# Turning the attended heads with VectorE's 32x32 block transposes, in a kernel of one gated attention stack

## The reference

```
x = x + tanh(g_xattn[0]) * divergence_attention_and_MLP(layernorm(x), ctx)      # phase a
x = x + tanh(g_ffn[0])   * linear(fp8(layernorm(x)), fp8(weight))               # phase b
x = x + tanh(g_xattn[1]) * attention(layernorm(x), ctx, mask, 16 heads of 16)   # phase b
x = x + tanh(g_ffn[1])   * (h + 0.5 * (silu(layernorm(h) @ w1 + b1) @ w2 + b2)) # phase b

# the attention, for each batch:
scores = q @ k.T / 4, where(mask == 0, -1e9); attn = softmax(scores)
out    = (attn @ value) by heads -> [256 tokens, 256] @ w_o.T + b_o
```

## Time and profile before

| | us |
|---|---|
| three runs: median (lowest to highest) | 1618.51 (1613.52 to 1624.93) |
| profiled execution, first to last instruction | 1614.4 |
| phase b in it | from about 600 on |
| one iteration with all eight letters | 27.8 |
| PE busy over the span | 1486.5 (92%) |
| DVE busy over the span | 1316.4 (82%) |
| ACT, POOL busy over the span | 1135.2, 1034.7 |

### The profile page before, as it was taken

One profiled execution on the slowest core, in us unless ns is written; L12 is line 12 of the kernel. 1 busy time (PEld: TensorE's weight loads), 2 busy tenths in 40 slices (PEclk: granted clock), 3 DMA queues, 4 the chain that ended last, 5 costly groups with the idle time before them and its releaser, 6 DMA issues.

```text
span 1614.4 us, 42641 instructions
## 1 busy us (share of the span) xinstructions
PE 1486.5 (92%) x14155; PEld 1144.6 (71%) x14155; DVE 1316.4 (82%) x3187; ACT 1135.2 (70%) x2057; POOL 1034.7 (64%) x1392
## 2 busy tenths in 40 slices
PE   4999999999999972668999999999999999999997
PEld 2788888888888861435667676777777776777666
DVE  4698888888888875778988889898988889898742
ACT  7798888888888742355666666666666666676664
POOL 4588888888888744224556565665656566565445
PEclk9999999999999995588999999999999999999999
DMA  7322222322222002332223232232223232232200
GB/s 228 96 80 66 91 72 65 96 66 69 93 65 71 2 1 92 80 119 73 80 80 87 73 85 80 85 87 81 83 78 92 72 91 74 86 85 84 64 16 22
DMA packets 197690, 125.45 MB, mean 78 GB/s; under 512 B 44400, under 2 KB 196848, under 8 KB 197360
## 3 DMA queue, kind: packets, MB, share of 16 engines
q1 hardware_dynamic: 197616, 124.48, 26.2%
HBM read 92.69 MB, written 25.17 MB: 73 GB/s over the span
## 4 chain that ended last, share of the span: by engine, by line
PE 48%; SPq 4%; DVE 3%; issue 2%; DMA 2%; POOL 2%; ACT 1%; POOLq 0%
PE b_bank L1835 28%; PE b_bank L1910 7%; PE b_scoreT L1892 4%; PE b_score L1875 4%; PE b_bank L1843 2%; PE b_bank L1987 1%; SPq L1306 1%; DMA b_nmT<-b_nm 1%; DMA b_yT<-b_y 1%; SPq L1290 1%; DVE b_nm L1653 1%; SPq L1279 1%; PE b_bank L1925 1%; ACT b_E L1471 1%; SPq L1315 0%
## 5 line engine op out<-in xcount | busy, mean ns | idle before, releaser
L1471 ACT ACTIVATE b_E<-b_scoreT 128x1024 f32<-128x1024 f32 x256 | 262.2, 1024 | 152.5 <-PE b_scoreT L1892 151.3
L1653 DVE TENSOR_REDUCE b_nm<-b_score 128x4 bf16<-128x1024 f32 x256 | 313.3, 1224 | 54.6 <-PE b_score L1875 48.4
L31 ACT ACT_TABLE_LOAD x157 | 201.4, 1283 | 18.6 <-PEq L1059 15.2
L1835 PE MATMUL b_bank<-f,b_YT 128*128 128x256 bf16 x1536 | 190.3, 274 | 4.7 <-POOL b_YT L1404 4.6
L890 PE MATMUL bank<-hT,W1T 128*128 128x256 bf16 x1536 | 183.3, 273 | 2.4 <-DVE hT L706 1.7
L1835 PE MATMUL b_bank<-b_hT,f 128*128 128x256 bf16 x1536 | 183.4, 273 | 0.8 <-DVE X L1749 0.8
L890 PE MATMUL bank<-W2T,G 128*128 128x256 bf16 x1024 | 171.0, 272 | 6.7 <-DVE GT L780 6.2
L1835 PEld LDWEIGHTS b_bank<-f,b_YT 128*128 128x128 bf16 x1536 | 143.5, 98 | 39.7 <-issue 19.5
L1835 PEld LDWEIGHTS b_bank<-b_hT,f 128*128 128x128 bf16 x1536 | 147.7, 98 | 30.3 <-issue 12.6
L890 PEld LDWEIGHTS bank<-hT,W1T 128*128 128x128 bf16 x1536 | 148.0, 98 | 27.7 <-ACT G L549 4.0
L1388 POOL TENSOR_TENSOR b_v<-b_v,b_e 128x512 f32<-128x512 f32 x32 | 40.6, 1269 | 195.0 <-DVE b_e L1734 195.0
(11 more groups left out here) (222 smaller groups left out, 3524.8 us busy)
## 6 DMA issues: line engine op xcount, KB each, us to landing
b_Q<-q_dram SPq DMA_DIRECT2D x192, 64.0 KB, 2.6
b_K<-k_dram SPq DMA_DIRECT2D x192, 64.0 KB, 2.8
xin<-in_x SPq DMA_DIRECT2D x32, 256.0 KB, 3.2
ctxn<-in_ctx SPq DMA_DIRECT2D x32, 256.0 KB, 2.8
mask_in<-in_mask SPq DMA_DIRECT2D x32, 256.0 KB, 3.0
X<-in_x SPq DMA_DIRECT2D x32, 256.0 KB, 4.0
ctxt<-in_ctxT SPq DMA_DIRECT2D x32, 256.0 KB, 4.2
b_ctxt<-in_ctxT SPq DMA_DIRECT2D x32, 256.0 KB, 2.8
```

Of the source, the lines that this page charges most:

```text
L31: act.add_instruction(mybir.InstLoadActFuncSet(name=nc.get_next_instruction_name(), act_func_set_id=which, ins=[], outs=[]))
L1471: nc.scalar.activation(E[:, pair:pair + 2], scoreT_ps[:, :, :, :], ACT.Exp).then_inc(sig["E"], 1)
L1653: nc.vector.tensor_reduce(pair, score_ps[:, :, :, :], AX.X, ALU.max, negate=True).then_inc(sig["nm"], 1)
L1835: last = nc.tensor.matmul(out_tile, lhs(i, k), rhs(j, k), start=start and k == chunks[0] and (i, j) == TERMS[0], stop=stop and k == chunks ...
```

## The change

The PE transposes of the attended heads and ACT's copies ahead of them go. DVE turns the tiles itself, in blocks of 32x32, out of PSUM (`heads_turned`), takes reciprocals and multiplies in SBUF (`inverse_sums`, `attended`), and turns the product back with a second block transpose (`heads_back`, tile `oF`). The rows of w_o and b_v are reordered on the way in so that the new order of the features fits. Half 0 of this is done in the iteration in which the batch is letter a, half 1 begins at the end of that iteration and ends in the next. Further, `statistics_2` stands ahead of maxima(5), `mlp_normalised` after maxima(6) of the iteration before, `scaled` right ahead of `binades`, `mask_bias` one letter earlier, and on POOL `inverse_std_2` ahead of `silu_parts`. The load of the mask goes from between the two steps on maxima to just behind the transposing transfers of `yT`.

```diff
             7: [("xT", "xlo", L_QKV, 1, 1), ("Q", "qlo", L_QKV, 1, 1), ("FFN", "ob", L_FFN, 1, 1),
                 ("PROJ", "x3", L_PROJ, 1, 1), ("H0", "Y", L_MLP, 4, 1), ("V", "V", L_QKV, 1, 1)],
-            8: [("OT0", "on", L_PROJ, 2, 1), ("hT", "hlo", L_MLP, 1, 1), ("ON", "onlo", L_PROJ, 1, 1),
-                ("AV01", "oS", L_ATT, 2, 1), ("H1", "Y", L_MLP, 4, 2)],
-            9: [("OT1", "on", L_PROJ, 2, 2), ("K", "klo", L_QKV, 1, 1), ("AV23", "oS", L_ATT, 2, 2),
-                ("H3", "Y", L_MLP, 4, 4)],
+            8: [("hT", "hlo", L_MLP, 1, 1), ("AV01", "at", L_ATT, 2, 1), ("H1", "Y", L_MLP, 4, 2)],
+            9: [("K", "klo", L_QKV, 1, 1), ("AV23", "at", L_ATT, 2, 2), ("H3", "Y", L_MLP, 4, 4)],
         }
...
                 if q:
+                    load_mask()
                     spill_queries()
...
                 if m:
                     transpose_maxima()
-                if q:
-                    load_mask()
...
-                if h:
-                    silu_parts(h, 0)
                 if f:
                     inverse_std_2()
                 if h:
+                    silu_parts(h, 0)
                     silu_parts(h, 1)
...
                 def attended_high():
-                    act.wait_ge(sig["onT_mm"], done(o))
+                    act.wait_ge(sig["oF"], done(o, per=C))
...
-                    nc.scalar.activation(oT[:, 0], whole_bank(BANK["ON"]), ACT.Copy).then_inc(sig["onhi"], 1)
-
-                def heads_copy(g):
...
+                    nc.scalar.activation(oT[:, 0], oF[:, :, :], ACT.Copy).then_inc(sig["onhi"], 1)
...
+                def heads_turned(c):
+
+                    dve.wait_ge(sig["av_mm"], done(a, per=NH // HG, part=2 * c + 2))
+                    nc.vector.transpose(at[:, 2 * c:2 * c + 2].rearrange("p g b r -> p (g b r)"),
+                                        flat_bank(BANK[("AV01", "AV23")[c]])).then_inc(sig["at"], 1)
+
+                def inverse_sums(c, b):
+                    dve.wait_ge(sig["at"], done(b, per=C, part=c + 1))
+                    nc.vector.reciprocal(rsum[:, 2 * c:2 * c + 2, :], at[:, 2 * c:2 * c + 2, :, DK]).then_inc(sig["rsum"], 1)
+
+                def attended(c, b):
+                    dve.wait_ge(sig["rsum"], done(b, per=C, part=c + 1))
+                    nc.vector.tensor_tensor(on[:, c].rearrange("p b g d -> p g b d"), at[:, 2 * c:2 * c + 2, :, 0:DK],
+                                            rsum[:, 2 * c:2 * c + 2, :].rearrange("p g (b u) -> p g b u", u=1).to_broadcast(
+                                                [P, 2, Q32, DK]), ALU.mult).then_inc(sig["on"], 1)
+
+                def heads_back(c, b):
+
+                    dve.wait_ge(sig["on"], done(b, per=C, part=c + 1))
+                    if (due := done(b, back=1)) is not None:
+                        dve.wait_ge(sig["onhi"], due)
+                    nc.vector.transpose(oF[:, c, :], on[:, c].rearrange("p b g d -> p (b g d)")).then_inc(sig["oF"], 1)
...
-                if h:
-                    mlp_normalised()
-                if n:
-                    scaled()
                 if o:
-                    attended(0)
+                    inverse_sums(1, o)
                 if m:
                     maxima(0)
+                if o:
+                    attended(1, o)
                 if q:
                     normalised_low()
                 if o:
-                    attended(1)
+                    heads_back(1, o)
...
                 if n:
+                    scaled()
                     binades()
...
+                if f:
+                    statistics_2()
                 if m:
                     maxima(5)
+                if a:
+                    heads_turned(0)
+                if m:
                     maxima(6)
+                if a:
+                    inverse_sums(0, a)
+                if o:
+                    mlp_normalised()
+                if a:
+                    attended(0, a)
                 if w:
                     result()
-                if f:
-                    statistics_2()
-                if m:
+                if a:
+                    heads_back(0, a)
+                if q:
                     mask_bias()
+                if m:
                     maxima(7)
                 if f:
                     attention_normalised()
+                if a:
+                    heads_turned(1)
...
-                if o:
-                    heads_transposed(0)
                 if m:
                     scores(0)
-                if o:
-                    heads_transposed(1)
...
-                if o:
-                    attended_transposed()
```

More of the change, by code:

```diff
@@ L1556, in iteration @@
                     exponential(6)
-                    heads_copy(0)
                     exponential(7)
@@ L1562, in iteration @@
                     silu(1)
-                if a:
-                    heads_copy(1)
                 if h:
@@ L1622, in mask_bias @@
                 def mask_bias():
-                    dve.wait_ge(sig[f"mask{m.parity}"], landed(m))
-                    if (due := done(m, back=2, per=NP)) is not None:
+                    dve.wait_ge(sig[f"mask{q.parity}"], landed(q))
+                    if (due := done(q, back=2, per=NP)) is not None:
                         dve.wait_ge(sig["scoreT_mm"], due)
-                    nc.vector.tensor_scalar(mb[m.parity][:, :, :], mask_in[:, :, :], 0.0, MINUS, ALU.is_equal,
+                    nc.vector.tensor_scalar(mb[q.parity][:, :, :], mask_in[:, :, :], 0.0, MINUS, ALU.is_equal,
                                             ALU.mult).then_inc(sig["mb"], 1)
                 def mlp_normalised():
-                    dve.wait_ge(sig["rs3"], done(h))
-                    if (due := done(h, back=1)) is not None:
+                    dve.wait_ge(sig["rs3"], done(o))
+                    if (due := done(o, back=1)) is not None:
                         dve.wait_ge(sig["hT_mm"], due)
                     for t in range(T):
-                        last = nc.vector.tensor_scalar(hn[:, t, :], Xb(h, t), mv3[:, t, 0:1], rh3[:, t:t + 1], ALU.subtract,
+                        last = nc.vector.tensor_scalar(hn[:, t, :], Xb(o, t), mv3[:, t, 0:1], rh3[:, t:t + 1], ALU.subtract,
                                                        ALU.mult)
@@ L1693, in keys_low @@
                     last.then_inc(sig["klo"], 1)
[L1695 to L1703, removed]
-                                            rsum[:, t, :].rearrange("p (h u) -> p h u", u=1).to_broadcast([P, NH, DK]),
-                                            ALU.mult).then_inc(sig["on"], 1)
+                def heads_turned(c):
+                    dve.wait_ge(sig["av_mm"], done(a, per=NH // HG, part=2 * c + 2))
+                    nc.vector.transpose(at[:, 2 * c:2 * c + 2].rearrange("p g b r -> p (g b r)"),
+                                        flat_bank(BANK[("AV01", "AV23")[c]])).then_inc(sig["at"], 1)
@@ L1797, in iteration @@
                     attention_update()
-                if m:
-                    maxima(5)
-                    maxima(6)
-                if w:
-                    result()
                 if f:
@@ L1980, in values_in @@
                     row_projection("V", 2, cT, "V_mm")
-                def heads_transposed(t):
-                    free(f"OT{t}")
-                    pe.wait_ge(sig["oS"], done(o, per=2))
-                    dst = flat_bank(BANK[f"OT{t}"])
-                    for g in range(NH // HG):
-                        last = nc.tensor.transpose(dst[:, tile(g)], oS[:, g, tile(t)], ident[:, :])
-                    last.then_inc(sig["oT_mm"], 1)
-                def attended_transposed():
-                    free("ON")
-                    pe.wait_ge(sig["on"], done(o, per=T))
-                    transposed(bank[BANK["ON"]], on, "onT_mm")
                 def output_projection():
@@ L2098, in col, with by_heads @@
         return np.ascontiguousarray(np.reshape(inputs[name], (-1, P)).T)
+    def by_heads(rows):
+        grid = np.reshape(rows, (2, 2, 4, DK, -1))
+        return np.ascontiguousarray(np.reshape(np.transpose(grid, (0, 2, 1, 3, 4)), (NH * DK, -1)))
     arrays = {
```

23 lines of the change are left out of this document (12 added, 11 removed).

## The result

| | before | after |
|---|---|---|
| median of four runs each (lowest to highest), us | 1617.62 (1613.52 to 1624.93) | 1677.42 (1675.11 to 1680.17) |
| profiled span, us | 1614.4 | 1673.2 |
| iterations with all eight letters, two lengths in turn, us | 27.80 and 27.93 | 29.98 and 30.2 |

The changed kernel is slower: ratio 1.0363, 95% interval 1.0333 to 1.0393. The forecast was 1663 us. Iterations of two lengths take turns in both kernels, and the forecast took the shorter one of before for all. The means are 27.87 and 30.1 us; the second length of before is seen from 1126.77 to

A forecast was written before the change was run, and what follows sets the result against it. PE bounds the kernel at 27.8 us an iteration; a loop of 29.4 + 0.2 = 29.6 us replaces it, 45 us over 25 iterations, hence 1663 us. Own range 1645 to 1685 (0.60); 8 in 10: 1622 to 1702.

The forecast's parts named there:

- the loop: Through bank 9: DVE's last transpose, `hidden(3)`, `values_in`, scores(0), maxima(0), DVE's work; 29.4 us, 29.6 with collisions.
- the second term: DVE from maxima(0) to the end of the last transpose: 26.0 less 0.27 for the reciprocal, 25.7 us.
- the 2.06 I kept: `xh` on DVE, two instructions beside POOL's work, assumed to take 2.06 us as before.
- 0.1 each: Loss of `attended` and `attended_low` to POOL, now reading both operands from SBUF: 0.2 us together.
- +3 and -4: Partly filled iterations: some 3 us more in neighbours of full ones, some 4 us back in the last.
- DVE's work, 26.0 us: DVE's work per iteration: 24.5 + 1.2 + 0.6 for block transposes - 0.3 for `v`'s new place.
- PE's, 26.3: PE's work per iteration: 27.8 us less 1.5 us of head transposes.
- `statistics_2` earlier ... costs nothing: On DVE: the move takes away the 1.4 us wait for `rs` and was costed at nothing.
- PE idle ahead of the fp8 matmuls: PE would wait some 0.8 us for `yT`, its way there being 1.5 us shorter and SP's not.
- PE as the bound: Rival: PE stays the bound, `yT` next, 27.4 us an iteration, faster at 1607 us; chance 0.11.
- `xh` came clear: Rival: `xh` avoids POOL, saving 1.3 us of the 1.8 per iteration, 1631 us; chance 0.13.
- Dearer collisions: Rival: transposes cost twice as much or both new SBUF pairs wait out POOL, about 1700 us; chance 0.16.

The follow-up runs named there:

- kernel 1: The changed kernel with DVE's block transpose that empties bank 9 ahead of `xh` instead of behind it: 1649.51 us, ratio 1.019.
- kernel 2: The changed kernel with ACT copying AV23 out of bank 9 and DVE's block transpose reading that copy: 1650.54 us, ratio 1.0191.
- kernel 9: Kernel 4 with `values_in` ahead of `hidden(2)` on PE and its copy ahead of `silu(2)` on ACT: 1634.60 us, ratio 1.0094.
- kernel 7: The changed kernel with `mask_bias` made for one column in 256 only: 1670.45 us, ratio 1.0313.
- kernel 4: The changed kernel with `statistics_2` behind maxima(5) instead of ahead of it: 1674.35 us, ratio 1.0348.
- kernel 3: The kernel before with the change's moves in the order alone, PE still turning the heads: 1649.71 us, ratio 1.0194.
- kernel 11: The changed kernel with ACT emptying bank 9, `statistics_2` behind maxima(5), `mask_bias` behind maxima(7), `values_in` ahead of `hidden(2)`, V's copy ahead of `silu(2)`: 1612.69 us, ratio 0.9966.
- kernel 8: The changed kernel with every moved step put back, so DVE's block transposes alone: 1698.70 us, ratio 1.0484.

## Why the prediction was right, and where its sum was short

The mechanism and the sign were right: the loop of kernels 1, 2 and 9. The forecast time was 14 us under the measured one. Its terms, in us of one iteration, measured from maxima(0) at 1132.79 to the next at 1162.88:

| step | forecast | measured |
|---|---|---|
| DVE, maxima(0) to the transpose's end, waits and collisions included, handing over | 25.7 + 0.5 + 0.1 + 0.2 = 26.5 | 26.83 (1132.79 to 1159.56, + 0.06) |
| `hidden(3)` and `values_in` | 2.62 | 2.72 (1159.62 to 1162.34) |
| scores(0) to maxima(0) | 0.44 | 0.54 (1162.34 to 1162.88) |
| sum | 29.6 | 30.09 |

- **What was mis-sized is the second term, and there several errors cancel.** `xh` took 1.13 for its two instead of the 2.06 I kept, 0.9 us in the change's favour. Against it: `mask_bias` took 1.07 us, 0.48 more than the mean of its two lengths before, and I had put its move at nothing; `attended` of half 1 took 0.72 and 0.82 in turn instead of 0.42 and `attended_low` 0.818 instead of 0.692, so 0.35 and 0.13 where I took 0.1 each; and the small transpose took 0.43, slot 0.35, above my bound of 0.34, the large one 0.704, slot 0.63 for 0.60. These come to nothing together: DVE's work is 26.1 us, forecast 26.2 with the collisions. What is left over is idle time of DVE inside the loop. It idles 30.1 - 26.1 = 4.0 us in an iteration, 3.0 of them ahead of maxima(0); the rest is 1.0, where I had put 0.6.
- **That the result lies in the range is in part luck.** With `xh` at its 2.06 us, and the rest as it came, an iteration would have been 0.9 us longer: some 23 us more, about 1700 by this estimate, and outside.
- **The 14 us.** The 25 full iterations, between the fifth and the thirtieth maxima(0), grew by 51.7 us (768.43 to 1468.49 before, 772.18 to 1523.94 after), where I had 45. Everything ahead of them grew by 4 us and everything behind by 3, together 7, where I had +3 and -4, together -1. So half of the 14 us lies in the full iterations and half in the partly filled ones: the time that I expected back at the end, once DVE is empty and PE has no heads to turn, did not show. Which step there holds it stays open.
- **Collisions with POOL are waits for the rest of a pass of POOL's that runs already, and then the instruction's own work.** Kernel 7 shows it for `mask_bias`, which reads one tile. `attended` fits: it took 0.42 us where it is clear; where it started at 1133.93 it took 0.82 and ended 0.28 us behind POOL's pass of 1133.31, as in every iteration from 900 to 1500 us. So the price goes by where in POOL's pass the instruction starts, and a median from a row in another place could not give it. The runs agree with the Trainium skill (SBUF — State Buffer, Who interferes with whom), by which the engine that issues first has the shared pair for the whole instruction; that section also lists `tensor_scalar`, the kind of `mask_bias`, among those that can take the pair when their operands allow it, which I did not apply to it.
- **DVE's work, 26.0 us:** 26.1. **PE's, 26.3:** 537.11/600 x 30.1 = 26.9. What would account for it is that each of four waits lets a group end by itself: `hidden(2)` is 1.48 us in its record and takes 1.32 where another group follows.
- **"`statistics_2` earlier ... costs nothing" failed.** In the changed kernel it happens to hold, 3 us by kernel 4, because the first loop is longer. In kernels 1, 2 and 3 it is the bound, at 29.0 to 29.2 us. I had asked only what waits at the place it left, and not what stands behind the place it came to: maxima(5), for which scores(6) waits.
- **PE idle ahead of the fp8 matmuls failed.** 0.3 us once in 600. SP's list before `yT` starts from maxima(7), and that is ahead of the late transpose on DVE: the transfers started 4.31 us behind `values_in` (1130.94 to 1135.25) and 4.94 before (1131.59 to 1136.53). Where the loops are cut the wait appears, as in kernel 11.
- **The waits foreseen:** PE's for `at` 0.88 us (forecast 1 to 2, and 1.82 once the second loop is out), DVE's ahead of maxima(0) 2.93 (nearly 3), DVE's busy share 87% in this stretch (88). Not foreseen: PE's two waits of 0.5 to 0.6 us for bank 7, which the first loop covers but for the 0.34 us by which scores(1) and so maxima(1) come late.
- **Rivals.** PE as the bound fell for the reason it was given. It takes both loops out of the way, and with them `mask_bias` and `values_in`, to come to 1612.69 us; the rival said 1607. `xh` came clear in part, and other instructions took what it gave. Dearer collisions were in part true; without what `xh` gave back they would have put the result outside the range.

The two loops do not add, since they share most of their work: the longer one sets the time. With 30.1 and 29.0 us, cutting the longer gives 28 us, the shorter alone 3, and both 36, until the transfer of the maxima is next at 28.7.

## What to carry to other kernels

When an engine takes over the emptying of a shared bank, walk the loop from that release through the other engine's queue back to the first engine's next step, and sum it: here it was 30.1 us while no engine had over 27. Then look for the second-longest loop before costing a moved step at nothing, and ask of its new place who waits for the instruction behind it. An instruction that is moved beside another engine's SBUF work should be priced by what is left of that engine's pass at its new place, plus its own work. Neither its median nor its longest row elsewhere would have done: `mask_bias` had 0.43 and 0.77, and took 1.07.

## What the runs showed of the hardware

- A block transpose of 32x32 in float32 took 0.704 us for 128x512 out of PSUM and 0.429 us for 128x256 in SBUF. The first is 0.02 us above the two-operand pass of the same shape; for the second the multiply of the same shape took 0.42.
- A DVE instruction of two elements per partition took 0.81 us where it started in a pass of POOL's (kernel 7), and ended 0.02 us behind the pass; the same with 512 elements took 1.07 us and ended 0.27 us behind it.
- In kernel 8 twelve matmuls took 2.51 us behind an idle time of 2.58 us, and 1.48 behind one of 2.53, and the iterations with the slow group are 1.3 to 1.8 us longer, but for one of 33.59. The granted clock, the last number but two, was 0.85 around the first and 1.00 around the second; from 900 to 1500 us it was 0.97, where the changed kernel, idle for 0.9 us there, had 1.00. Why the clock falls behind one such wait and not behind the next I did not test.

```profile
1110.00:1118.00 8.00, 5.42 (x51) 3.55 (x44) 6.63 (x13) 1.03 (x3) 4.01 (x6) 0.85 0.32 88
1142.00:1150.00 8.00, 5.42 (x59) 3.73 (x48) 6.21 (x11) 1.92 (x5) 3.85 (x6) 1.00 0.30 81
```
